# Expert layer: first weight tiles rounded between the logit copies, logits turned ahead of tokens, last rows copied by two engines, output in eight pieces

## The chip, the cores and the metric

The kernel is one program on one core of a Trainium2 chip. The core has a matrix engine (TensorE, PE), a vector engine (VectorE, DVE), a scalar engine (ScalarE, ACT), GpSimd (POOL) and SyncE (SP), whose queue issues all transfers here. Each engine takes its instructions in program order, and they wait for each other by semaphores. TensorE writes to PSUM, eight banks of 128 x 512 fp32 values. The metric is the time of one execution on the device in microseconds (us), less is better.

## What is computed

A decoder of six layers on x (2 x 1024 tokens of 256 features): linear attention, cross attention to a context, a recurrence, causal attention, cross attention, and a layer of eight experts. Only the last matters here:

```python
x = inputs.reshape(G, S, Mm)                 # 8 groups of 256 tokens, 256 features
logits = jnp.einsum('GSM,ME->GSE', x, router_w)          # 8 experts
dispatch, combine = _gating_top2(logits, C)              # softmax, two best experts, 64 slots
expert_inputs = jnp.einsum('GSEC,GSM->EGCM', dispatch, x)
layer_w0 = jnp.einsum('EGCM,EMH->EGCH', expert_inputs, w0_kernel)     # H = 1368
layer_w1 = jnp.einsum('EGCM,EMH->EGCH', expert_inputs, w1_kernel)
hidden = jax.nn.gelu(layer_w0, approximate=True) * layer_w1
expert_outputs = jnp.einsum('EGCH,EHM->EGCM', hidden, wo_kernel)
out = jnp.einsum('EGCM,GSEC->GSM', expert_outputs, combine)           # added to x
```

`inputs` is the layer-normalised residual stream, and the result is added to that stream.

## The kernel before

Everything lies with features on partitions and tokens along the row; `c.xT` is the residual stream, two feature halves (FT = 2) by 2048 tokens. All that follows is `expert_layer`. Its order is written out by hand, engine by engine; there is no scheduler.

**Router.** For each of four chunks of 512 tokens `flat_logits` multiplies the normalised tokens by the router's weights into a bank of 8 rows, ScalarE copies them to `flat` (`copy_flat`), and `turn_logits` transposes them so that tokens are on partitions. VectorE reads the turned logits of all chunks at once and makes softmax and two choices in small steps (`do`), with one Exp by ScalarE; two groups of matmuls (`table`) count how many tokens chose an expert before, and the slot codes follow.

**Tokens.** Meanwhile each pair of token tiles is transposed (`turn_x`, eight pairs), rounded by ScalarE to the matrix format (`split_tokens`, into `tok_high`), and the remainder is made by TensorE (`leave_rest`) and copied by ScalarE (`rest_of_tokens`, `tok_rest`). High part and rest together keep fp32 precision.

**Gather.** For each 128 tokens VectorE writes a one-hot tile in two operations (L3161 and L3163, `one_part` and `one_hot`, double-buffered by group). For each of eight groups of 256 tokens `gather` multiplies them with tokens (L2834, four matmuls for each of two feature halves), and ScalarE copies the slots (L3065, L3067). The first gather needs the codes and the rest of all tokens.

**Weights.** An expert's weights come in three parts by SyncE's queue, those of expert 0 at the layer's start. ScalarE rounds a tile of w0 and w1 (`split_w`, L2991, 128 x 512), and GpSimd subtracts to get the rest (`rest_of_w`, L2794). Five tiles (AHEAD = 5) are done ahead of the loop. SyncE asks for the next expert's first part once GpSimd has subtracted the fourth tile.

**Loop.** 88 units (8 experts, 11 tiles of the hidden dimension): `widen` (12 matmuls, L2885), Gelu by ScalarE, product by VectorE, rounding by ScalarE and rest by GpSimd, and two units later `narrow` (6 matmuls, L2898). Besides, pairs of experts are combined in two banks used in turn (`ring_bank`): tiles called `e` are an expert's output transposed to slots (two for each expert), `y` are their products with the turned gates, added to `c.xT` by VectorE (L3203).

**Tail.** After the last expert come the tiles of `last`: two `e` tiles (L2910), each copied by VectorE in two halves of 64 rows (L3214, rows of the two experts interleaved), and eight `y` tiles (L2922), of four token ranges q by two feature halves m. Each `y` first waits for the copy of the second `e` tile, and for its bank to have been read. SyncE stores each 512 tokens (both halves, 512 KB) when its second sum has been added.

The program's names: `psum` banks, `arena` a shared buffer (normalised tokens, `flat`, slots, `e_out`), `m_...` the tiles of this layer.

Of the kernel before, what the change touches and what calls it, by code (L numbers as in the profile page):

```python
# [25 lines left out]
ACT = mybir.ActivationFunctionType  # L26
# [5 lines left out]
FT = D // P  # L32
CH = 512
# [26 lines left out]
EXP, HID, CAP, GR = 8, 1368, 64, 8  # L60
# [2581 lines left out]
def expert_layer(nc, c):  # L2642
# [3 lines left out]
    PAIRS = EXP // 2  # L2646
    GP = GR // 2
# [5 lines left out]
    AHEAD, W_RING = 5, 6  # L2653
# [24 lines left out]
    with ExitStack() as ctx:  # L2678
# [4 lines left out]
        e = c.signals(nc, "e", dict(made=0, read=0, w0_done=0, w1_done=0, gelu=0, hidden=0, h_high=0, h_rest=0, comb=0, combined=0,  # L2683
                                       narrowed=0, out_copied0=0, out_copied1=0, x_high=0, x_rest=0, w_high=0, w_rest=0, o_high=0,
                                       o_rest=0, w_loaded0=0, w_loaded1=0, w_loaded2=0, wo_loaded0=0, wo_loaded1=0, wo_loaded2=0,
                                       stored=0, router=0))
        set_round(0, s, e)
        w_loaded = [e[f"w_loaded{g}"] for g in range(len(PARTS))]
        wo_loaded = [e[f"wo_loaded{g}"] for g in range(len(PARTS))]
# [23 lines left out]
        router = sb("m_router", [P, FT, EXP])  # L2713
# [41 lines left out]
        with nc.Block() as block:  # L2755

            @block.sync
            def _(sync):
                at = c.mats["router"][0]
                sync.dma_start(router[:].rearrange("p k e -> p (k e)"), c.weights_dram[:, at:at + FT * EXP]).then_inc(e["router"].sem, 16)  # L2760
                for g in range(len(PARTS)):
                    load_first(sync, 0, g)
                    load_last(sync, 0, g)
                for ex in range(1, EXP):
                    for g in range(len(PARTS)):
                        sync.wait_ge(*e["w_rest"](HT * (ex - 1) + PARTS[g][-1] + 1))
                        load_first(sync, ex, g)
                        sync.wait_ge(*e["o_rest"](HT * (ex - 1) + PARTS[g][-1] + 1))
                        load_last(sync, ex, g)
                for q in range(GP):  # L2770
                    sync.wait_ge(*e["read"](nth["y", PAIRS - 1, q, FT - 1] + 1))
                    sync.dma_start(c.out[:, :, q * CH:(q + 1) * CH], c.xT[:, :, q * CH:(q + 1) * CH]).then_inc(e["stored"].sem, 16)
                sync.wait_ge(*e["stored"](GP * 16))

            @block.gpsimd
            def _(pool):
# [34 lines left out]
            def _(pe):  # L2811
# [4 lines left out]
                def tile(what):  # L2816
                    n = nth[what]
                    if n >= BANKS:
                        pe.wait_ge(*e["read"](n - BANKS + 1))
                    return ring_bank(what)  # L2820

                def gather(g, m):
# [29 lines left out]
                def turn_x(t2):  # L2852
                    if t2 >= TURNS:
                        pe.wait_ge(*s["x_high"](t2 - TURNS + 1))
                    for t in (0, 1):
                        for k in range(FT):
                            mm = pe.transpose(turn_bank(t2)[:, t * D + k * P:t * D + (k + 1) * P],  # L2857
                                              tokens(k, 2 * t2 + t), c.ident[:])
                    mm.then_inc(s["turned"].sem)

                def leave_rest(t2):

                    pe.wait_ge(*s["x_high"](t2 + 1))
                    if t2 >= 2:
                        pe.wait_ge(*s["x_rest"](t2 - 1))
                    pe.matmul(rest_bank(t2), minus[:], two(tok_high, t2), start=True, stop=False)
                    for t in (0, 1):
                        for k in range(FT):
                            mm = pe.matmul(rest_bank(t2)[:, t * D + k * P:t * D + (k + 1) * P],  # L2869
                                           tokens(k, 2 * t2 + t), c.ident[:],  # L2870
                                           start=False, stop=(t == 1 and k == FT - 1))
                    mm.then_inc(s["x_left"].sem)
# [29 lines left out]
                def fill(what):  # L2902
                    bank = tile(what)
                    if what[0] == "e":
                        _, ex, i = what
                        for m in range(FT):
                            pe.wait_ge(*out_copied[m](ex + 1))
                        for q in (0, 1):
                            for m in range(FT):
                                mm = pe.transpose(bank[:, q * D + m * P:q * D + (m + 1) * P],  # L2910
                                                  out_t[:, m, (2 * i + q) * P:(2 * i + q + 1) * P], c.ident[:])
                    elif what[0] == "back":
                        _, j, q = what
                        pe.wait_ge(*e["combined"](j + 1))
                        for t in range(4):
                            mm = pe.transpose(bank[:, t * P:(t + 1) * P], comb[:, 4 * q + t, :], c.ident[:])  # L2916
                    else:
                        _, j, q, m = what
                        pe.wait_ge(*e["read"](nth["e", 2 * j + 1, 1] + 1))
                        for i in range(2):  # L2920
                            g = 2 * q + i
                            mm = pe.matmul(bank[:, i * D:(i + 1) * D], e_out[:, g, m * P:(m + 1) * P],  # L2922
                                           back[:, g * 2 * P:(g + 1) * 2 * P], start=True, stop=True)
                    mm.then_inc(e["made"].sem)
# [14 lines left out]
                turn_x(0)  # L2939
                for j in LATE:  # L2940
                    flat_logits(j)
                for t2 in range(1, 3):
                    turn_x(t2)
                    if t2 == 1:
                        pe.wait_ge(*s["negated"](1))
                    leave_rest(t2 - 1)
                for j in LATE:
                    turn_logits(j)
                for t2 in range(3, 6):
                    turn_x(t2)  # L2950
                    leave_rest(t2 - 1)
                pe.wait_ge(*s["consts"](2))
# [32 lines left out]
            def _(act):  # L2985
                def split_w(n):
                    ex, h = divmod(n, HT)
                    act.wait_ge(*w_loaded[part_of(h)](2 * 16 * (ex + 1)))
                    if n >= W_RING:
                        act.wait_ge(*e["w1_done"](n - W_RING + 1))  # L2990
                    act.activation(w_high[:, n % W_RING, :, :, 0:H_N(h)], raw_of(n), ACT.Copy).then_inc(e["w_high"].sem)  # L2991
# [38 lines left out]
                def copy_flat(j):  # L3030
                    act.wait_ge(*s["flat"](j + 1))
                    act.activation(flat[:, j * CH:(j + 1) * CH], c.bank(j % 2)[0:EXP, :], ACT.Copy).then_inc(s["flat_copied"].sem)

                def split_tokens(t2):
                    act.wait_ge(*s["turned"](t2 + 1))
                    act.activation(two(tok_high, t2), turn_bank(t2), ACT.Copy).then_inc(s["x_high"].sem)

                def rest_of_tokens(t2):
                    act.wait_ge(*s["x_left"](t2 + 1))
                    act.activation(two(tok_rest, t2), rest_bank(t2), ACT.Copy).then_inc(s["x_rest"].sem)  # L3040

                copy_flat(0)
                copy_flat(1)
                split_tokens(0)
                copy_flat(2)
                copy_flat(3)
                for t2 in (1, 2):
                    split_tokens(t2)
                    rest_of_tokens(t2 - 1)
                act.wait_ge(*s["step"](2))  # L3050
                act.activation(tab["raw"][:], tab["raw"][:], ACT.Exp).then_inc(s["step"].sem)
                for t2 in range(3, TIL // 2):
                    split_tokens(t2)
                    rest_of_tokens(t2 - 1)
                rest_of_tokens(TIL // 2 - 1)
                for n in range(AHEAD):
                    split_w(n)
                for g in range(GR):
                    for m in range(FT):
                        n = FT * g + m  # L3060
# [11 lines left out]
                for n in range(UNITS):  # L3072
# [12 lines left out]
                    if ex + 1 < EXP and h == 6:  # L3085
                        split_x(ex + 1)
                copy_out(EXP - 1)

            @block.vector
            def _(dve):  # L3090
# [107 lines left out]
                def empty(what):  # L3198
                    of = tile(what)
                    if what[0] == "y":  # L3200
                        _, j, q, m = what
                        x = c.xT[:, m, q * CH:(q + 1) * CH]
                        dve.tensor_tensor(x, of, x, ALU.add).then_inc(e["read"].sem)  # L3203
                    elif what[0] == "back":
                        _, j, q = what
                        dve.tensor_copy(back[:, q * CH:(q + 1) * CH], of).then_inc(e["read"].sem)
                    else:

                        _, ex, i = what
                        of = of.rearrange("p (q n) -> p q n", q=2)  # L3210
                        to = e_out[:, 4 * i:4 * i + 4, :].rearrange("p (q g) n -> p q g n", g=2)
                        for side in range(2):
                            rows = slice(side * CAP, (side + 1) * CAP)
                            ins = dve.tensor_copy(to[rows, :, side ^ (ex % 2), :], of[rows])  # L3214
                        ins.then_inc(e["read"].sem)
# [283 lines left out]
```

## Time and profile before

| | us |
|---|---|
| median of three runs | 1656.48 |
| lowest and highest | 1653.85, 1660.80 |
| profiled execution, its own time | 1651.91 |
| its span in the profile | 1650.2 |
| TensorE busy in the span | 1533.0 (93%) |
| VectorE busy | 962.3 (58%) |
| ScalarE busy | 718.6 (44%) |
| GpSimd busy | 372.2 (23%) |

Times in the views are microseconds from the start of the span. A matmul's record overlaps the next one's, since they are pipelined; the chain of waits shows their share without overlap. "Idle before" is how long an engine did nothing before a row, with what ended it. The granted clock is a share of TensorE's full 2.4 GHz. The expert layer runs from 1175 us to the end.

### The profile page before, as it was taken

The page shows a single profiled execution, that of the slowest core. Times are in us where ns is not written, and L with a number is a line of the kernel's source. Part 1 is how long each engine was busy: PE and PEld are TensorE (multiplying, and loading weights), DVE is VectorE, ACT ScalarE, POOL GpSimd, SP SyncE. Part 2 cuts the span into 40 slices and gives each one's busy share as a digit, 9 for nine tenths or more (in the row PEclk, how much of TensorE's full clock was granted, in tenths as well). Part 3 has the DMA queues.
Part 4 walks back from the last instruction along what each step waited for, and adds up shares of the span by engine and source line. Part 5 has one row for each costly group of instructions (what it writes and reads, how often), then busy time and mean ns, then how long its engine had stood idle before and what let it go on. Part 6 is the DMA issues. An engine that isn't in the chain of part 4 may idle for free. (4 is left out here: it accounts for less than half of the span.)

```text
span 1650.2 us, 19104 instructions
## 1 busy us (share of the span) xinstructions
PE 1533.0 (93%) x6998; PEld 838.9 (51%) x7002; DVE 962.3 (58%) x1491; ACT 718.6 (44%) x1256; POOL 372.2 (23%) x300
## 2 busy tenths in 40 slices
PE   6989999998999999977999999889879999999998
PEld 3744444432222234434454544332358888888886
DVE  4642124767675652343978776368579575564753
ACT  4345232453334333251466566533555444545441
POOL 0000000122221210034200000110216655655561
PEclk9989999999999999987999999989999999999998
DMA  6000000000000000017255330000302332312201
GB/s 274 1 1 0 0 0 4 1 0 1 1 0 1 1 0 0 0 68 98 28 128 67 40 40 2 1 4 1 103 26 77 98 100 73 103 65 88 84 9 51
DMA packets 38707, 67.54 MB, mean 41 GB/s; under 512 B 3864, under 2 KB 19288, under 8 KB 38232
## 3 DMA queue, kind: packets, MB, share of 16 engines
q1 hardware_dynamic: 38616, 66.33, 15.6%
q8 instruction: 56, 0.92, 0.2%
q14 instruction: 35, 0.29, 0.1%
HBM read 57.80 MB, written 8.39 MB: 40 GB/s over the span
## 5 line engine op out<-in xcount | busy, mean ns | idle before, releaser
L1994 ACT ACTIVATE arena<-psum 128x512 f32<-128x512 f32 (+3 forms) x384 | 164.8, 498 | 131.0 <-PE psum L1863 97.5
L2051 DVE TENSOR_REDUCE b_mx<-psum 128x1 f32<-128x512 f32 (+3 forms) x304 | 181.3, 653 | 44.3 <-PE psum L1841 34.8
L2794 POOL TENSOR_TENSOR m_w_rest<-m_w,m_w_high 128x512 fp32r<-128x512 f32 (+1 forms) x88 | 112.6, 1281 | 159.4 <-ACT m_w_high L2991 159.4
L3230 DVE TENSOR_TENSOR m_hidden<-m_gelu,psum 128x512 f32<-128x512 f32 (+1 forms) x88 | 60.4, 686 | 143.6 <-ACT m_gelu L3079 122.5
L2885 PE MATMUL psum<-m_x_high,m_w_high 128*128 128x512 f32 (+1 forms) x352 | 137.2, 390 | 2.9 <-issue 2.9
L2885 PE MATMUL psum<-m_x_rest,m_w_high 128*128 128x512 f32 (+1 forms) x352 | 137.0, 389 | 0.0
L2885 PE MATMUL psum<-m_x_high,m_w_rest 128*128 128x512 f32 (+1 forms) x352 | 137.0, 389 | 0.0
L2800 POOL TENSOR_TENSOR m_h_rest<-m_hidden,m_h_high 128x512 fp32r<-128x512 f32 (+1 forms) x88 | 122.0, 1387 | 58.0 <-ACT m_h_high L3005 58.0
L1203 ACT ACTIVATE x_probs<-psum 128x1024 f32<-128x1024 f32 x64 | 65.5, 1023 | 135.9 <-PE psum L955 135.9
L1346 DVE TENSOR_REDUCE x_mx<-psum 128x2 f32<-128x1024 f32 x64 | 77.0, 1219 | 51.2 <-PE psum L929 51.1
L3079 ACT ACTIVATE m_gelu<-psum 128x512 f32<-128x512 f32 (+1 forms) x88 | 52.4, 596 | 119.0 <-PE psum L2885 119.0
L1838 PE MATMUL psum<-b_k_stack,b_q_stack 96*128 96x512 bf16 (+3 forms) x288 | 89.4, 341 | 6.5 <-POOL weights_sb L1770 3.7
L1860 PE MATMUL psum<-b_q_stack,b_k_stack 98*128 98x512 bf16 (+3 forms) x288 | 90.0, 331 | 5.4 <-DMA b_q_stack<-b_stage 3.1
L3005 ACT ACTIVATE m_h_high<-m_hidden 128x512 fp32r<-128x512 f32 (+1 forms) x88 | 55.7, 633 | 81.5 <-DVE m_hidden L3230 81.5
L968 PE MATMUL psum<-x_probs,arena 128*64 128x512 f32 x256 | 71.0, 633 | 8.5 <-ACT x_out L1213 8.5
L955 PE MATMUL psum<-arena 64*128 64x512 f32 x256 | 74.8, 662 | 0.0
L2885 PEld LDWEIGHTS psum<-m_x_high,m_w_high 128*128 128x128 f32 (+1 forms) x352 | 65.0, 185 | 17.9 <-issue 3.2
L1875 PE MATMUL psum<-arena,weights_sb 128*32 128x512 f32 (+3 forms) x768 | 73.3, 500 | 0.0
L2885 PEld LDWEIGHTS psum<-m_x_high,m_w_rest 128*128 128x128 f32 (+1 forms) x352 | 65.0, 185 | 15.0
L2885 PEld LDWEIGHTS psum<-m_x_rest,m_w_high 128*128 128x128 f32 (+1 forms) x352 | 65.0, 185 | 14.9
L2898 PE MATMUL psum<-m_h_high,m_o_high 128*128 128x512 f32 (+1 forms) x176 | 72.3, 411 | 0.2 <-POOL m_h_rest L2800 0.2
L2898 PE MATMUL psum<-m_h_high,m_o_rest 128*128 128x512 f32 (+1 forms) x176 | 68.8, 391 | 0.0
(546 smaller groups left out, 3008.1 us busy)
## 6 DMA issues: line engine op xcount, KB each, us to landing
m_w<-w SPq DMA_DIRECT2D x32, 512.0 KB, 4.6
m_wo<-wo SPq DMA_DIRECT2D x16, 512.0 KB, 3.9
weights_sb<-weights SPq DMA_DIRECT2D x2, 2820.0 KB, 12.2
m_w<-w SPq DMA_DIRECT2D x16, 344.0 KB, 5.0
b_q_stack<-b_q_dram SPq DMA_DIRECT2D x36, 128.0 KB, 6.8
b_k_stack<-b_k_dram SPq DMA_DIRECT2D x36, 128.0 KB, 7.3
weights_sb<-weights SPq DMA_DIRECT2D x1, 3328.0 KB, 13.6
b_q_dram<-b_q_parts SPq DMA_DIRECT2D x6, 512.0 KB, 3.7
```

What stands on the lines that cost most here:

```text
L955: mm = pe.matmul(to[0:keys, h, :], k, qt[b][rows, m, half * CH:(half + 1) * CH], start=False, stop=True)
L968: mm = pe.matmul(out_tile[h * DH:(h + 1) * DH, :], v, probs[slot % RING][0:keys, h, :], start=(kt == 0), stop=(kt == TT))
L1346: dve.tensor_reduce(mx[:, n % 2, i // 2, i % 2, :], two_heads(tile(("piece", n, i))), AX, ALU.max).then_inc(s["read"].sem)
L1838: mm = pe.matmul(bank[:, x * keys:(x + 1) * keys], qs[n % 3][0:ROWS, h, qi * P:(qi + 1) * P], ks[n % 3][0:ROWS, h, first:first + keys], st ...
L1860: mm = pe.matmul(score(slot)[:, 0:n], ks[a][0:ROWS + SHIFT, h, ki * P:(ki + 1) * P], qs[a][0:ROWS + SHIFT, h, q0:q0 + n], start=True, stop ...
L1875: mm = pe.matmul(out_tile[h * PAD:(h + 1) * PAD, CH - n:CH], v_aug[:, b * TT + ki, quad * QUAD + h, :], probs[(QUAD * (2 * pair + i) + h) ...
L1994: act.activation(probs[slot % RING][:, 0:n], score(slot)[:, 0:n], ACT.Exp, scale=SCALE).then_inc(s["expd"].sem)
L2051: dve.tensor_reduce(mx[:, part, qi, heads[0]:heads[0] + nh], tile(("piece", p))[:, 0:nh * keys].rearrange("p (h n) -> p h n", n=keys), AX, ...
L2794: pool.tensor_tensor(w_rest[:, n % W_RING, :, :, 0:H_N(n % HT)], raw_of(n), w_high[:, n % W_RING, :, :, 0:H_N(n % HT)].bitcast(F32), ALU.s ...
L2800: pool.tensor_tensor(h_rest[rows, n % H_RING, :], hidden[rows, n % 2, :], h_high[rows, n % H_RING, :].bitcast(F32), ALU.subtract).then_inc ...
L2885: mm = pe.matmul(c.bank(base + n % 2)[0:H_N(h), :], of[:, k, :], x_of[ex % 2][:, k, :], start=(k == 0 and i == 0), stop=(k == FT - 1 and i ...
L2898: mm = pe.matmul(total(m), of[rows, n % O_RING, m * P:(m + 1) * P], h_of[rows, n % H_RING, :], start=(h == 0 and i == 0), stop=(h == HT - ...
```

## The change

Five weight tiles are rounded by ScalarE between the logit copies instead of behind the last token copy. TensorE turns the last logits right after the second turn of tokens. In the tail, ScalarE copies rows 64 to 127 of the last two `e` tiles, with a semaphore `half_read` of its own, and a product waits only for the `e` tile that it reads. The output is stored in eight pieces, one for each `y` tile. Nothing of the arithmetic changes.

```diff
@@ SyncE
-                    sync.wait_ge(*e["read"](nth["y", PAIRS - 1, q, FT - 1] + 1))
-                    sync.dma_start(c.out[:, :, q * CH:(q + 1) * CH], c.xT[:, :, q * CH:(q + 1) * CH]).then_inc(e["stored"].sem, 16)
-                sync.wait_ge(*e["stored"](GP * 16))
+                    for m in range(FT):
+                        sync.wait_ge(*e["read"](nth["y", PAIRS - 1, q, m] + 1))
+                        sync.dma_start(c.out[:, m, q * CH:(q + 1) * CH], c.xT[:, m, q * CH:(q + 1) * CH]).then_inc(e["stored"].sem, 16)
+                sync.wait_ge(*e["stored"](GP * FT * 16))
@@ TensorE, a bank for a tile
                         pe.wait_ge(*e["read"](n - BANKS + 1))
+                        if what[0] == "y" and what[1] == PAIRS - 1 and what[2] == 0:
+                            pe.wait_ge(*e["half_read"](what[3] + 1))
@@ TensorE, a y tile
-                        pe.wait_ge(*e["read"](nth["e", 2 * j + 1, 1] + 1))
+                        pe.wait_ge(*e["read"](nth["e", 2 * j + 1, q // 2] + 1))
+                        if j == PAIRS - 1:
+                            pe.wait_ge(*e["half_read"](q // 2 + 1))
@@ TensorE, router
-                for t2 in range(1, 3):
-                    turn_x(t2)
-                    if t2 == 1:
-                        pe.wait_ge(*s["negated"](1))
-                    leave_rest(t2 - 1)
+                turn_x(1)
                 for j in LATE:
                     turn_logits(j)
-                for t2 in range(3, 6):
+                pe.wait_ge(*s["negated"](1))
+                leave_rest(0)
+                for t2 in range(2, 6):
                     turn_x(t2)
                     leave_rest(t2 - 1)
@@ ScalarE, router
                 copy_flat(1)
+                for n in range(2):
+                    split_w(n)
                 split_tokens(0)
+                split_w(2)
                 copy_flat(2)
+                split_w(3)
                 copy_flat(3)
-                for t2 in (1, 2):
-                    split_tokens(t2)
-                    rest_of_tokens(t2 - 1)
+                split_w(4)
+                split_tokens(1)
+                rest_of_tokens(0)
+                split_tokens(2)
+                rest_of_tokens(1)
...
-                for n in range(AHEAD):
-                    split_w(n)
@@ ScalarE, tail
                 copy_out(EXP - 1)
+                for what in last[:2]:
+
+                    _, ex, i = what
+                    act.wait_ge(*e["made"](nth[what] + 1))
+                    rows = slice(CAP, 2 * CAP)
+                    to = e_out[:, 4 * i:4 * i + 4, :].rearrange("p (q g) n -> p q g n", g=2)
+                    act.activation(to[rows, :, 1 ^ (ex % 2), :], ring_bank(what).rearrange("p (q n) -> p q n", q=2)[rows], ACT.Copy)\
+                       .then_inc(e["half_read"].sem)
@@ VectorE, an e tile
-                        for side in range(2):
+                        for side in range(1 if ex == EXP - 1 else 2):
```

ScalarE's queue in the router, of the kernel before, from the first two logit copies (`arena<-psum 8x512`) to Exp (`m_raw`):

```order
L3032 ACTIVATE arena<-psum 8x512 x2
L3036 ACTIVATE m_tok_high<-psum 128x512
L3032 ACTIVATE arena<-psum 8x512 x2
L3036 ACTIVATE m_tok_high<-psum 128x512
L3040 ACTIVATE m_tok_rest<-psum 128x512
L3036 ACTIVATE m_tok_high<-psum 128x512
L3040 ACTIVATE m_tok_rest<-psum 128x512
L3051 ACTIVATE m_raw<-m_raw 128x128
```

The same stretch of the changed kernel, whose line numbers are 3 to 9 higher:

```order
L3035 ACTIVATE arena<-psum 8x512 x2
L2994 ACTIVATE m_w_high<-m_w 128x512 x2
L3039 ACTIVATE m_tok_high<-psum 128x512
L2994 ACTIVATE m_w_high<-m_w 128x512
L3035 ACTIVATE arena<-psum 8x512
L2994 ACTIVATE m_w_high<-m_w 128x512
L3035 ACTIVATE arena<-psum 8x512
L2994 ACTIVATE m_w_high<-m_w 128x512
L3039 ACTIVATE m_tok_high<-psum 128x512
L3043 ACTIVATE m_tok_rest<-psum 128x512
L3039 ACTIVATE m_tok_high<-psum 128x512
L3043 ACTIVATE m_tok_rest<-psum 128x512
```

Five `m_w_high` stand ahead of the second token tile; Exp still comes after two `m_tok_rest`. TensorE's queue of the kernel before, from the last two chunks' logits (`m_router`) to the turned logits (`128x8`):

```order
L2843 MATMUL psum<-arena,m_router 8x512 x4
L2857 MATMUL psum<-ident,arena 128x128 x4
L2866 MATMUL psum<-m_tok_high,m_minus 128x512
L2869 MATMUL psum<-ident,arena 128x128 x4
L2857 MATMUL psum<-ident,arena 128x128 x4
L2866 MATMUL psum<-m_tok_high,m_minus 128x512
L2869 MATMUL psum<-ident,arena 128x128 x4
L2849 MATMUL psum<-ident,arena 128x8 x8
```

And of the changed kernel, the same matmuls:

```order
L2846 MATMUL psum<-arena,m_router 8x512 x4
L2860 MATMUL psum<-ident,arena 128x128 x4
L2852 MATMUL psum<-ident,arena 128x8 x8
L2869 MATMUL psum<-m_tok_high,m_minus 128x512
L2872 MATMUL psum<-ident,arena 128x128 x4
L2860 MATMUL psum<-ident,arena 128x128 x4
L2869 MATMUL psum<-m_tok_high,m_minus 128x512
L2872 MATMUL psum<-ident,arena 128x128 x4
```

The turned logits pass two groups of `leave_rest` (a matmul with `m_minus` and four with tokens) and one turn of tokens.

## Rows read from the trace of the kernel before

**Rows 1.** The page's first line: span and number of instructions.
```profile
span 1650.2 us, 19104 instructions
```

**Rows 2.** Windows: busy time (x records) by engine, granted clock, DMA share, GB/s.
```profile
1190.00:1195.00 5.00, 5.00 (x37) 3.67 (x35) 0.00 (x0) 2.86 (x6) 0.00 (x0) 1.00 0.00 0
1215.00:1220.00 5.00, 3.94 (x10) 2.63 (x9) 4.86 (x8) 1.32 (x4) 1.37 (x1) 0.50 0.67 210
1240.00:1640.00 400.00, 396.33 (x1804) 325.94 (x1803) 248.51 (x402) 186.05 (x364) 225.68 (x171) 0.99 0.22 72
1638.00:1640.00 2.00, 2.00 (x6) 1.62 (x5) 0.99 (x2) 0.00 (x0) 0.00 (x0) 0.50 0.00 0
```

**Rows 3.** Timeline, TensorE, 1200 to 1237: start, us, operation, count, idle before.
```profile
1201.45 0.46 PE L2955 MATMUL psum<-m_m,m_before 128*128 128x128 f32 x2 [1.45 <-DVE m_t L3136]
...
1208.70 0.47 PE L2834 MATMUL psum<-m_one_hot,m_tok_high 128*128 128x512 f32 x1 [1.07 <-DVE m_one_hot L3163]
...
1213.94 0.47 PE L2834 MATMUL psum<-m_one_hot,m_tok_high 128*128 128x512 f32 x1 [3.18 <-DVE m_one_hot L3163]
...
1224.37 0.47 PE L2834 MATMUL psum<-m_one_hot,m_tok_high 128*128 128x512 f32 x1 [0.74 <-issue]
...
1231.48 0.47 PE L2834 MATMUL psum<-m_one_hot,m_tok_high 128*128 128x512 f32 x1 [0.28 <-issue]
...
1236.39 0.47 PE L2885 MATMUL psum<-m_x_high,m_w_high 128*128 128x512 f32 x1 [2.85 <-issue]
```

**Rows 4.** One line's instructions: count, shortest/median/longest in ns, first and last start.
```profile
L3161 DVE TENSOR_SCALAR arena<-m_iota,m_code x16: 476/481/1509, 1206.1 to 1230.1; 128x512 f32<-128x512 f32 x16
```
```profile
L3163 DVE SCALAR_TENSOR_TENSOR m_one_hot<-m_iota,m_code,arena x16: 750/752/1689, 1206.7 to 1230.6; 128x512 fp32r<-128x512 f32 x16
```

**Rows 5.** Timeline of VectorE: the normalising, and three rows of the gather.
```profile
1185.25 2.50 DVE L3111 TENSOR_TENSOR arena<-arena 128x512 f32<-128x512 f32 x4 [3.94 <-ACT arena L3028]
...
1209.03 1.69 DVE L3163 SCALAR_TENSOR_TENSOR m_one_hot<-m_iota,m_code,arena 128x512 fp32r<-128x512 f32 x1
...
1221.81 0.49 DVE L3161 TENSOR_SCALAR arena<-m_iota,m_code 128x512 f32<-128x512 f32 x1 [1.33 <-PE psum L2834]
```

**Rows 6.** Timeline of GpSimd, the five subtractions ahead of the loop.
```profile
1208.87 7.50 POOL L2794 TENSOR_TENSOR m_w_rest<-m_w,m_w_high 128x512 fp32r<-128x512 f32 x5 [30.75 <-ACT m_w_high L2991]
```

**Rows 7.** Timeline of ScalarE: the last residue copy before Exp, and the roundings.
```profile
1194.60 0.60 ACT L3040 ACTIVATE m_tok_rest<-psum 128x512 fp32r<-128x512 f32 x1 [0.48 <-PE psum L2869]
...
1208.17 2.70 ACT L2991 ACTIVATE m_w_high<-m_w 128x512 fp32r<-128x512 f32 x5
```

**Rows 8.** Chain of waits in the router: start, us without overlap, what.
```profile
1191.28 0.59 PE psum L2857 x4
...
1194.57 0.60 PE psum L2849 x8
...
1196.16 0.32 ACT m_raw L3051
```

**Rows 9.** Timeline of the tail, all engines.
```profile
1631.26 0.60 ACT L3017 ACTIVATE m_out_t<-psum 128x512 f32<-128x512 f32 x1 [3.17 <-PE psum L2898]
...
1632.76 2.81 DVE L3214 COPY arena<-psum 64x512 f32<-64x512 f32 x4 [0.81 <-PE psum L2910]
...
1635.72 10.25 PE L2922 MATMUL psum<-arena 128*128 128x256 f32 x32 [2.56 <-DVE arena L3214]
1637.80 0.69 DVE L3203 TENSOR_TENSOR xT<-psum,xT 128x512 f32<-128x512 f32 x1 [2.23 <-PE psum L2922]
...
1642.18 0.69 DVE L3203 TENSOR_TENSOR xT<-psum,xT 128x512 f32<-128x512 f32 x1 [0.27 <-PE psum L2922]
...
1646.01 0.69 DVE L3203 TENSOR_TENSOR xT<-psum,xT 128x512 f32<-128x512 f32 x1 [0.27 <-PE psum L2922]
```

**Rows 10.** DMA issues: count, KB each, median us from issue to landing.
```profile
out<-xT SPq DMA_DIRECT2D x4, 512.0 KB, 3.1
...
x_cx<-ctx_t SPq DMA_DIRECT2D x1, 128.0 KB, 2.2
```

More of the change, by code:

```diff
@@ L2685, in expert_layer @@
                                        o_rest=0, w_loaded0=0, w_loaded1=0, w_loaded2=0, wo_loaded0=0, wo_loaded1=0, wo_loaded2=0,
-                                       stored=0, router=0))
+                                       stored=0, router=0, half_read=0))
         set_round(0, s, e)
```

## The prediction

> **What bounds the kernel now.** I read the page's span first [rows 1], then the windows [rows 2]: from 1240 to 1640 us TensorE is busy 396.33 of 400 us. That loop over experts is at its bound, and nothing in the change takes a matmul out of it. The time can move only where TensorE waits: in the router and gather ahead of the loop (1186 to 1236 us) and in the tail (after 1631 us). So I read the timelines of both, engine by engine.
>
> The router is one chain: logits turned, a row of small VectorE steps with one Exp by ScalarE among them, slot codes, then 16 pairs of VectorE operations (L3161, L3163) that write the one-hot tiles, two pairs for each of the eight gathers by TensorE. Ahead of the last four gathers VectorE sets the pace: gathers 4 and 7 start at 1224.37 and 1231.48 us [rows 3], so (1231.48 - 1224.37) / 3 = 2.37 us for each. Their eight matmuls stand 0.31 us short of that. Gather 0 starts at 1208.70, so at this pace gather 7 would start at 1208.70 + 7 x 2.37 = 1225.29. It starts 6.19 us later.
>
> The rows say why. L3161 takes 476 to 481 ns mostly and 1509 at most, L3163 750 and 1689 [rows 4]; the long ones are those from 1209.03 on [rows 5], exactly while GpSimd does its first five subtractions L2794 (1208.87, 7.50 us in all) [rows 6]. Those wait for ScalarE's five roundings of weights, L2991, which stand behind the last copy of tokens (1208.17 us, 2.70 us) [rows 7]. Then TensorE, left waiting, runs at a granted clock of 0.50, its 1.2 GHz level, between 1215 and 1220 us [rows 2], and VectorE in turn idles 1.33 us at 1221.81 for it [rows 5].
>
> **Part 1, five weight tiles rounded earlier.** ScalarE's five L2991 move between the logit copies, to about 1186.7 us on. Each takes 2.70 / 5 = 0.54 us of queue; the gaps ahead of the logit copies hold them, except that the last stands ahead of the second token tile. GpSimd can then subtract from about 1187.4: five of 7.50 / 5 = 1.50 us at most, over by 1195. In the gather VectorE keeps its short durations. Gain: the 6.19 us above. The other half of the double buffer has to follow: the pair for gather 2 waits for gather 0's matmuls, 2.06 us after 1208.70, and in my timetable it wants to start only 0.1 us after that; the rows of gathers 4 to 7 have the same order and keep 2.37 us. I take the full 6.19; the lower bound, if only the durations shrink and the clock still falls, is 6.19 - 1.33 = 4.86.
>
> What do the moved subtractions hit? VectorE's normalising, L3111, ends at 1187.75 (1185.25 + 2.50) [rows 5]; then it idles until the logits. With logits at 1192.5 (part 2) three small steps stand before Exp, about 1 us. Were each held for as long as L3161's worst excess (1509 - 481 = 1028 ns) Exp's input would be ready at 1196.6; but GpSimd is through by 1195, so it is ready by 1195.5 at the latest, and Exp isn't reached before 1195.7 (below). Cost 0. If that cover goes, it costs up to 0.9 us.
>
> The weights must have landed. No DMA moves between 1190 and 1195 us [rows 2], so all have; ScalarE wants the first at 1186.7. A landing as late as 1190 would cost up to 3.3 us; the first megabyte of 5.3 requested is in my view there long before. Cost 0. SyncE, which waits on GpSimd's fourth subtraction, asks for expert 1's first weights some 20 us earlier; nobody waits for the queue then.
>
> **Part 2, logits turned ahead of tokens.** Before, two residue groups and a turn of tokens stood ahead of the last turned logits, from the end of the turn at 1191.87 to 1194.57 [rows 8]: 2.70 us. Now the last logits are turned at 1192.47. But Exp, which the chain needs next, stands on ScalarE behind two token copies and two residue copies. The last of these waits for TensorE's second residue group, which now ends at 1194.57 + 0.60 = 1195.17 (the turned logits ahead of it). That copy started at 1194.60 before [rows 7]; now it starts at 1195.20, and Exp some 0.52 behind it, at 1195.72 instead of 1196.16 [rows 8]. **Gain 0.44, not 2.70.** TensorE's work up to the counts is the same sum and ends at 1200.0, as before (1201.45 less 1.45 idle) [rows 3]; VectorE's steps now reach the counts at 1200.9, so the 0.44 survives. Bounds: 0 (ScalarE loses 0.4 to the queue) and 1.45 (TensorE is the limit).
>
> From gather 7 to the first widening matmul lie 1236.39 - 1231.48 = 4.91 us [rows 3]: same operations, same order, unchanged. **Ahead of the loop: 6.19 + 0.44 = 6.6 us.**
>
> **Part 3, last rows by two engines.** Before, VectorE makes four copies, 2.81 us from 1632.76 [rows 9], and TensorE's last products start at 1635.72. Now VectorE copies rows 0 to 63 and ScalarE rows 64 to 127 of each bank. ScalarE's comparable copy of 128 x 512 takes 0.60 us [rows 9], shorter than VectorE's 2.81 / 4 = 0.70, so VectorE's first ends last, 1633.46. The first product needs only the first bank: it starts at 1633.60. **Gain 2.12.** No row shows both engines reading one bank at once; if they took turns each bank would cost 0.6 more, and 1.5 of the 2.12 is left; I take 0 for that, as the halves are different partitions. The memory page bears on it: by the Trainium skill (PSUM — Partial Sum Buffer, on bank collisions) two engines may be in one bank at once when they are in different 32-partition quadrants, which these are; no run here shows it, and by that rule the sum would be the one I take.
>
> Second, the clock. TensorE stood idle before 1635.72 and ran at 0.50 at 1638 to 1640 [rows 2]. The first sum was read 2.08 us after the start (1637.80), against half of that, 1.04, at 2.4 GHz; and after 1642.18 the sums are read every (1646.01 - 1642.18) / 4 = 0.96 us [rows 9]. With the idle 2.56 us cut to about 0.4 I expect no fall: start to last read is 1.04 + 7 x 0.96 = 7.76 instead of 10.29. **Gain 2.5**; the lower bound is 0, if it falls all the same.
>
> **Part 4, output in eight.** After the last addition (1646.70) 3.5 us are left. 512 KB land in 3.1 us; the nearest smaller one, 128 KB, in 2.2 [rows 10]. A piece of 256 KB by the straight line: 2.5. **Gain 0.6**, between 0 and 0.9. The issue, about 0.55 us before, fits into the 0.96 between sums. Removing one wait and adding two on TensorE (`half_read`) queues nothing else behind them.
>
> **Sum.** 6.19 + 0.44 + 2.12 + 2.53 + 0.6 = 11.9 us. The profiled execution has 1651.91 us (span 1650.2), so it would come to 1640.0. The median of the three runs shown is 1656.48, 4.6 higher; its terms are the same, so I take off the same: **1644.6 us**, 0.72% less.
>
> **Rivals.**
> *The tail's clock falls all the same.* For it: part of the idle time ahead of it stays. Against: its longest stretch, 2.56 us, goes. Gain 9.4: 1647.1 us. 15%.
> *The clock falls ahead of the loop instead.* TensorE idles 2.85 us before the first widening, and no fall shows there now, but a slightly longer one at 1213.94 (3.18 us) did bring one [rows 2, 3]; the shift of all by 6.6 us may do it. Half speed for about as long as it lasted, 6.6 us, costs 3.3: 1647.9 us. 8%.
> *The collision moves with the subtractions.* If ScalarE or the weights are late, GpSimd's five land in the small VectorE steps: 5 x 1.03 = 5.1 back, 1649.7 us. Against: the idle from 1187.75 to 1192.5. 7%. By the Trainium skill (SBUF — State Buffer, "Who interferes with whom") a VectorE operation with two SBUF inputs, or a fast copy or tensor_scalar, and a GpSimd one hold the shared port for a whole instruction, and a reduction never does. L3161's 1509 against 481 ns agrees. By it only the subtraction of the maxima would be held before Exp, and the result is as in part 1; were the five late, fewer than five steps would be held and the loss is smaller than 5.1.
> *Slower: the weights' landing becomes the bound.* ScalarE is in order, so a wait for weights now stops logits and tokens behind it, where it stopped nothing before. Each microsecond past 1186.7 goes on the chain. It eats the whole gain from a landing at 1198.6 on; at 1204 the kernel takes 1661.9 us. Against: DMA is idle by 1190. 2%.
> *The turning does nothing,* ScalarE's queue holding Exp altogether: 1645.0, inside my own range.
>
> **How the numbers follow.** Forecast with small misses of its terms 63%, clock in tail 15, clock before the loop 8, collision 7, slower 2, the rest (5) for a median of three runs that themselves spread over 7 us. About 0.5%, 8.3 us, is what a measurement of this kernel can tell; the line stands at 1648.2. Faster by more: 63 + 15 + most of 8, less a few for the spread: 0.81. Within: 0.17. Slower: 0.02. Low end: forecast less the 1 us that TensorE's slack would allow and some 3 of spread, 1640.5. High end: the collision case, 1650.
>
> **What would show it.** Right: all 16 pairs in the gather near 0.48 and 0.75 us; gathers 2.37 apart at clock 1.00; GpSimd's first five over before Exp; logits read 2.7 us earlier but Exp only 0.4; last products starting 2.1 us sooner, relative to the last narrowing; sums 0.96 apart throughout. Wrong: long L3161 rows anywhere, a gap on TensorE before gather 2, Exp gaining the whole 2.7, ScalarE's half-copies slower than 0.7 us, or clock 0.50 in either place.

## Result and profile after

The changed kernel takes 1643.88 us (median of ten runs, 1637.78 to 1649.77), the kernel before 1655.07 (ten runs, 1649.85 to 1661.16). The ratio of the runs is 0.9936, 95% interval 0.9916 to 0.9955; of 1655.07 us that is 10.6 us less (7.4 to 13.9), while the two medians alone differ by 11.2. The forecast was 1644.6 and 11.9 us less.

The profiled executions differ by only 8.0 us (span 1642.2 against 1650.2), because the changed kernel reaches its expert layer 4.1 us later, in code that is the same. In the recurrence, 390 to 510 us, the granted clock was 1.00 before and is 0.92 and 0.94 now. Counted by VectorE's instructions, which are the same in both, the changed kernel falls 8.5 us behind in this stretch, and regains a part of it later. The windows of the kernel before, and below them of the changed kernel (busy time and count of five engines, granted clock, DMA share, GB/s):

```profile
390.00:450.00 60.00, 53.86 (x254) 15.72 (x252) 46.15 (x49) 19.72 (x21) 11.82 (x6) 1.00 0.00 1
450.00:510.00 60.00, 57.93 (x254) 16.28 (x252) 42.39 (x45) 21.05 (x22) 14.64 (x7) 1.00 0.00 1
```
```profile
390.00:450.00 60.00, 54.30 (x238) 15.43 (x236) 42.56 (x45) 17.03 (x17) 9.85 (x5) 0.92 0.00 0
450.00:510.00 60.00, 58.36 (x238) 15.97 (x238) 39.21 (x42) 19.49 (x20) 14.10 (x6) 0.94 0.00 1
```

So I count from the first router matmul (1182.48 us before, 1186.57 now). All numbers are differences between starts in the timelines, in us:

| stretch | before | changed | difference | forecast |
|---|---|---|---|---|
| router to VectorE's read of the logits | 12.71 | 10.02 | -2.69 | -2.7 |
| router to Exp | 13.68 | 13.40 | -0.28 | -0.44 |
| router to gather 0 | 26.22 | 25.92 | -0.30 | -0.44 |
| gather 0 to gather 7 | 22.78 | 16.58 | -6.20 | -6.19 |
| gather 7 to the first widening | 4.91 | 4.94 | 0.03 | 0 |
| loop, to the last unit's narrowing | 393.21 | 393.22 | 0.01 | 0 |
| to the first product | 6.12 | 4.11 | -2.01 | -2.12 |
| to the last sum's start | 10.29 | 7.75 | -2.54 | -2.53 |
| to the end of the span | 4.19 | 3.11 | -1.08 | -0.6 |
| router to the end of the span, the sum | 467.72 | 455.63 | -12.09 | -11.9 |

The first rows answer [rows 3 to 5]. One line of the changed kernel each, L3176 and L3178 (count, shortest/median/longest in ns), and VectorE's three steps before Exp:

```profile
L3176 DVE TENSOR_SCALAR arena<-m_iota,m_code x16: 478/480/486, 1209.9 to 1227.7; 128x512 f32<-128x512 f32 x16
```
```profile
L3178 DVE SCALAR_TENSOR_TENSOR m_one_hot<-m_iota,m_code,arena x16: 750/751/752, 1210.5 to 1228.2; 128x512 fp32r<-128x512 f32 x16
```
```profile
1196.59 0.29 DVE L3129 COPY m_logits<-psum 128x128 f32<-128x128 f32 x1 [4.75 <-PE psum L2852]
1196.91 0.29 DVE L3132 TENSOR_REDUCE m_mx<-m_logits 128x16 f32<-128x128 f32 x1
1197.23 0.81 DVE L3133 TENSOR_TENSOR m_raw<-m_logits,m_mx 128x128 f32<-128x128 f32 x1
1200.37 0.29 DVE L3136 TENSOR_REDUCE m_sm<-m_raw 128x16 f32<-128x128 f32 x1 [2.33 <-ACT m_raw L3060]
```

No long one-hot operation is left. Beside GpSimd's subtractions now stand these steps instead: the row of GpSimd's timeline below (it answers [rows 6]) ends at 1197.90, and the one step with two inputs in SBUF, L3133, took 0.81 instead of 0.29 us, while the copy from PSUM and the reduction kept 0.29. It cost nothing: after it VectorE still waited 2.33 us for Exp. By the Trainium skill (SBUF — State Buffer, "Who interferes with whom") just this kind of step contends with a GpSimd instruction that reads SBUF, and a reduction never does; the trace agrees, with these numbers.

```profile
1191.40 6.50 POOL L2795 TENSOR_TENSOR m_w_rest<-m_w,m_w_high 128x512 fp32r<-128x512 f32 x5 [9.19 <-ACT m_w_high L2994]
```

ScalarE's queue around Exp (its L3060), answering [rows 7, 8], and the chain of waits there:

```profile
1197.91 0.60 ACT L3043 ACTIVATE m_tok_rest<-psum 128x512 fp32r<-128x512 f32 x1 [0.91 <-PE psum L2872]
1198.40 0.59 ACT L3039 ACTIVATE m_tok_high<-psum 128x512 fp32r<-128x512 f32 x1
1199.47 0.60 ACT L3043 ACTIVATE m_tok_rest<-psum 128x512 fp32r<-128x512 f32 x1 [0.48 <-PE psum L2872]
1199.97 0.30 ACT L3060 ACTIVATE m_raw<-m_raw 128x128 f32<-128x128 f32 x1
```
```profile
1195.96 0.59 PE psum L2852 x8
1196.55 0.43 PE psum L2869
...
1199.47 0.60 ACT m_tok_rest L3043
1200.07 0.20 ACT m_raw L3060
```

Exp starts right behind the second residue copy, with its input long there. The tail, answering [rows 9, 10]; ScalarE's and VectorE's half copies start together, and the clock holds:

```profile
1630.40 1.28 DVE L3229 COPY arena<-psum 64x512 f32<-64x512 f32 x2 [0.81 <-PE psum L2913]
1632.48 0.69 DVE L3218 TENSOR_TENSOR xT<-psum,xT 128x512 f32<-128x512 f32 x1 [0.80 <-PE psum L2927]
```
```profile
1630.40 1.08 ACT L3101 ACTIVATE arena<-psum 64x512 f32<-64x512 f32 x2 [0.91 <-PE psum L2913]
```
```profile
1632.00:1636.00 4.00, 4.00 (x19) 2.83 (x18) 2.77 (x4) 0.00 (x0) 0.00 (x0) 1.00 0.36 137
1636.00:1640.00 4.00, 3.05 (x14) 2.03 (x12) 2.77 (x4) 0.00 (x0) 0.00 (x0) 1.00 0.74 279
```
```profile
out<-xT SPq DMA_DIRECT2D x8, 256.0 KB, 2.0
```

### The profile page after: what moved, and what is told of

Same layout as the page of the kernel before. It is cut to its first block and busy times, and to the rows that moved or that the text cites. A ratio compares the mean times of both kernels' runs of the same rounds, so it can differ in the third digit from the quotient of the medians.

```text
span 1642.2 us, 19114 instructions
## 1 busy us (share of the span) xinstructions
PE 1530.5 (93%) x7002; PEld 835.0 (51%) x7002; DVE 957.0 (58%) x1489; ACT 719.7 (44%) x1258; POOL 371.3 (23%) x300
```

## Experiments

My theory: GpSimd's subtractions beside the one-hot operations cost 6.2 us; the early logits are held by ScalarE's queue; the tail gained by shorter copies and, separately, by the clock. The rivals stand in each expectation. Times of timed runs are compared with runs of the kernel before on the same chip. Five of the kernels (logits alone, output alone, subtractions late, tail kept busy, Exp moved up) have one execution each: they are read from their traces, by stretches, and their whole times say nothing.

**One part at a time.** First the roundings alone: ScalarE's lines of the diff ahead of this, TensorE's order and the tail left as before.

> The kernel before with one part of the change alone: the five roundings of weights stand between the logit copies; the logits are turned where they were, the tail is the old one. Theory (GpSimd's five subtractions hold VectorE's one-hot operations, and that starves TensorE until its clock falls): gather 0 to gather 7 takes 16.6 us instead of 22.8 (a gain of 6.2), all one-hot operations stay near 0.48 and 0.75 us, the clock stays 1.00, and the time is 0.996 of that before. The path up to gather 0 is unchanged or up to 0.3 us longer, since a rounding stands ahead of the second token tile. Rival (the gain in front comes from the logits being turned early): gather 0 to gather 7 stays within 0.5 us of 22.8, and the time stays at 1.000.

Gather 0 to gather 7 took 16.57 us, router to gather 0 26.22, as before; ratio 0.9959 (0.9934 to 0.9984). This part is the larger one, and the rival falls. Two other stretches differ in this profile, though nothing was changed in them: the loop took 394.84 us and not 393.2, and the tail's products 9.27 and not 10.29; more on both below.

The logits alone:

```diff
-                for t2 in range(1, 3):
-                    turn_x(t2)
...
-                    leave_rest(t2 - 1)
+                turn_x(1)
                 for j in LATE:
                     turn_logits(j)
+                pe.wait_ge(*s["negated"](1))
+                leave_rest(0)
...
```

> The kernel before with only the logits turned ahead of the token groups on TensorE. Theory: VectorE reads the logits 2.7 us earlier after the first logit matmul, but Exp on ScalarE stands behind the second residue copy and comes only 0.3 to 0.5 us earlier, as do the counts and gather 0; gather 0 to gather 7 stays at 22.8 us with the long one-hot operations. Rival (Exp follows the logits): Exp 2.7 us earlier, counts 1.4 us earlier, where TensorE is the limit.

Logits at 10.02, Exp at 13.40, gather 0 at 25.94, gather 0 to 7 in 22.33 us. As the theory has it.

The tail copies alone (ScalarE's, VectorE's and TensorE's lines of the tail, output in four):

> The kernel before with only the new tail copies: ScalarE copies rows 64 to 127 of the last two transposed tiles, a product waits only for its own tile, output in four pieces as before. Theory: last narrowing to first product 4.1 us instead of 6.1 (gain 2.0), first product to last sum read 7.8 instead of 10.3 (gain 2.5, the clock stays 1.00), last read to the end unchanged at 4.2; together 4.5 us, 0.997 of the time before. Rival (the clock falls in the tail whenever the idle stretches add up, and stayed up in the changed kernel by chance): gain 2.0 only and the clock at 0.50 in the products.

Narrowing to first product 4.11 us, products 7.75, end 4.15; ratio 0.9978 (0.9954 to 1.0003), an interval that takes in no change, so the 4.5 us rest on the trace. In this run the clock fell elsewhere: the loop took 396.09 us.

The output alone:

```diff
-                    sync.wait_ge(*e["read"](nth["y", PAIRS - 1, q, FT - 1] + 1))
-                    sync.dma_start(c.out[:, :, q * CH:(q + 1) * CH], c.xT[:, :, q * CH:(q + 1) * CH]).then_inc(e["stored"].sem, 16)
+                    for m in range(FT):
+                        sync.wait_ge(*e["read"](nth["y", PAIRS - 1, q, m] + 1))
+                        sync.dma_start(c.out[:, m, q * CH:(q + 1) * CH], c.xT[:, m, q * CH:(q + 1) * CH]).then_inc(e["stored"].sem, 16)
```

> The kernel before with only the output stored in eight pieces. Theory: from the start of the last sum to the end of the span 3.1 us instead of 4.2 (issue 0.33 instead of 0.53, landing 2.0 instead of 3.1); the rest of the tail as before, products at clock 0.50 for about 6 us. Rival (the last piece queues behind the one ahead of it, and only the faster tail made the changed kernel's end short): 3.7 us or more.

From the last sum to the end of the span it takes 3.10 us, with the old slow tail ahead of it (products in 10.12). So the 1.1 us belong to the piece's size.

**Is it GpSimd's subtraction, or ScalarE's queue?** The changed kernel, with one wait more:

```diff
+                pool.wait_ge(*s["one"](2))
                 for n in range(AHEAD):
                     rest_of_w(n)
```

> The changed kernel, in which GpSimd starts its five subtractions only once the first pair of one-hot tiles is written, as in the kernel before; ScalarE's roundings stay early. Theory (the subtractions beside the one-hot operations are the cause, and ScalarE's order is not): one-hot operations of 1.5 to 1.7 us return, the clock falls, and gather 0 to gather 7 takes 21 to 23 us instead of 16.6. Rival (ScalarE's roundings between token copies and slot copies were the cause, since slot copies free the banks): it stays at 16.6 us.

Gather 0 to 7 took 22.90 us, though ScalarE had rounded early. GpSimd's subtractions and VectorE's one-hot operations in this run:

```profile
1208.00 7.65 POOL L2795 TENSOR_TENSOR m_w_rest<-m_w,m_w_high 128x512 fp32r<-128x512 f32 x5 [30.28 <-DVE m_one_hot L3179]
```
```profile
1207.83 0.48 DVE L3177 TENSOR_SCALAR arena<-m_iota,m_code 128x512 f32<-128x512 f32 x1
1208.35 1.66 DVE L3179 SCALAR_TENSOR_TENSOR m_one_hot<-m_iota,m_code,arena 128x512 fp32r<-128x512 f32 x1
1209.93 1.49 DVE L3177 TENSOR_SCALAR arena<-m_iota,m_code 128x512 f32<-128x512 f32 x1
```

The first long operation is the first one that starts after GpSimd has (1208.35 against 1208.00); the one that was already running kept its 0.48 us. That settles the cause: the overlap in time, and not ScalarE's order. Nor are transfers a rival for the long operations: in the kernel before, four of them fill this window, GpSimd is busy throughout, and no DMA moves (the share before the last number is 0.00):

```profile
1210.00:1215.00 5.00, 1.82 (x8) 1.19 (x7) 4.96 (x4) 1.96 (x6) 5.00 (x5) 0.96 0.00 0
```

The loss in the gather has two parts. In each of the six profiles with late subtractions five one-hot operations are long, and they last 4.7 to 4.8 us more in sum than short ones. In the profile with the output alone, gather 0 to 7 took 21.33 us, which is 16.57 and just this sum, although the clock fell there too. In the other five it took 1.0 to 1.6 us more, which is what is left for TensorE at the lower clock.

**Is the tail's slowness the clock?** The kernel before, with TensorE kept at work:

```diff
                 for what in last:
+                    if what == ("y", PAIRS - 1, 0, 0):
+                        pe.wait_ge(*e["gelu"](UNITS))
+                        for _ in range(10):
+                            pe.matmul(c.bank(0), w_high[:, 0, 0, 0, :], x_high[1][:, 0, :], start=True, stop=True)
                     fill(what)
```

> The kernel before with ten more matmuls of 128 x 512 on TensorE between the last transposes and the first product, into a bank that nobody reads; all else as before. Theory (idle time of TensorE lowers its clock in the tail): the products still start 6.1 us after the last narrowing begins, but the clock stays 1.00 there, and the first product to the last sum read takes 7.8 us instead of 10.3. Rival (the products are slow for another reason, such as VectorE's reads or the last copies): 10.3 us as before.

The products start 6.14 us after the narrowing, as before, and take 7.75. TensorE's timeline, and a window at clock 1.00:

```profile
1638.78 2.54 PE L2985 MATMUL psum<-m_x_high,m_w_high 128*128 128x512 f32 x10
1641.59 7.71 PE L2922 MATMUL psum<-arena 128*128 128x256 f32 x32 [0.27 <-DVE arena L3218]
```
```profile
1640.00:1644.00 4.00, 3.73 (x16) 2.68 (x15) 2.50 (x5) 0.00 (x0) 0.00 (x0) 1.00 0.00 0
```

Ten matmuls that nobody reads bring 2.5 us: TensorE's idle time was the cause, and the slow copies mattered by making it. This is one execution, but the other profiles agree: the clock was at 0.50 in the products in all four with the old tail and nothing in its wait, and at 1.00 up to the last sum in all seven with the new tail.

**What the early logits could be worth.** The changed kernel, with Exp moved up on ScalarE:

```diff
                 rest_of_tokens(0)
+                act.wait_ge(*s["step"](2))
+                act.activation(tab["raw"][:], tab["raw"][:], ACT.Exp).then_inc(s["step"].sem)
                 split_tokens(2)
                 rest_of_tokens(1)
-                act.wait_ge(*s["step"](2))
-                act.activation(tab["raw"][:], tab["raw"][:], ACT.Exp).then_inc(s["step"].sem)
```

> The changed kernel with Exp on ScalarE ahead of the third token copy and the second residue copy. Theory (ScalarE's queue kept the early logits from helping): Exp about 1.5 us earlier than in the changed kernel, counted from the first logit matmul, and the counts and gather 0 about 1.1 earlier, since TensorE's own work then is the limit (no idle time ahead of the counts). Rival (Exp's input was late, not its queue): Exp and gather 0 within 0.3 us of the changed kernel.

Exp at 11.83 (1.57 earlier than in the changed kernel), counts at 17.41 instead of 18.67, gather 0 at 24.59 instead of 25.92: 1.3 us, where I expected about 1.1. Then also the counts:

```diff
-                turn_x(6)
-                leave_rest(5)
                 pe.wait_ge(*s["cum2"](1))
...
                 mm.then_inc(s["cnt"].sem)
+                turn_x(6)
+                leave_rest(5)
                 turn_x(7)
...
                         pe.wait_ge(*s["codes"](2))
+                    if n == 2:
                         pe.wait_ge(*s["x_rest"](TIL // 2))
```

> As the one with Exp ahead, and the matmuls of the second choice's counts stand ahead of the seventh turn of tokens, and the first gather no longer waits for the rest of the last tokens (the second one does). Theory: TensorE has no idle stretch left up to the first gather, which starts 1.9 us earlier than in the changed kernel; the gathers stay 2.37 us apart, so the loop starts 1.9 us earlier, and the time is 0.9925 of that before, against 0.9936 of the changed kernel. Rival (gathers are then held by the last residue copies): gather 1 waits and 1 us or less is gained.

Gather 0 at 23.48 us, 2.44 earlier than in the changed kernel, where I expected 1.9, and gather 0 to 7 in 16.54. Ratio to the kernel before 0.9909 (0.9882 to 0.9935).

**The wait ahead of the loop.** On top of that, ScalarE rounds the first half of expert 0's tokens sooner:

```diff
+                        if g == GR - 1:
+                            act.wait_ge(*s["gathered"](n + 1))
+                            act.activation(x_high[0][:, m, :], x_slots[m][:, 0, :], ACT.Copy).then_inc(e["x_high"].sem)
-                act.wait_ge(*s["gathered"](GR * FT))
-                split_x(0)
```

> As the one with Exp and counts ahead, and ScalarE rounds the first half of expert 0's tokens as soon as the last gather's first half is copied, instead of behind the second half. Theory: the stretch from gather 7's start to the first widening matmul is 4.3 us instead of 4.93, so TensorE idles 2.2 us there instead of 2.85; a loop of 393.2 us (clock 1.00 from the start) becomes likelier against 394.8. Rival (something else, such as the rounding of the output weights or the table load of Gelu, ends that wait): 4.9 us as before.

The stretch is 4.57 us instead of 4.93, a little over half of the gain I expected; TensorE idles 2.48 us there, and the clock fell all the same; the loop took 394.82. Ratio 0.9904 (0.9873 to 0.9934). Then the gap filled:

```diff
+                pe.wait_ge(*e["w_high"](1))
+                for _ in range(8):
+                    pe.matmul(c.bank(5), minus[:], w_high[:, 0].rearrange("p w k n -> p (w k n)"), start=True, stop=True)
                 pe.wait_ge(*s["gathered"](GR * FT))
```

> As the one before it, with eight more matmuls of 128 x 512 on TensorE (1.8 us at full clock, into a bank that nobody reads) in the wait ahead of the loop. Theory (the loops of 394.8 and 396.1 us are those in whose first microseconds the clock is at its lower level, since TensorE idled ahead of them): the clock is 1.00 there and the loop takes 393.2 us; the time is at or below that of the kernel with Exp and counts ahead, 0.990 of that before. Rival (the longer loops have another cause): 394.8 or more stays possible with clock 1.00 at the start.

The loop took 393.22 us. Windows of TensorE early in the loop without the fill (the loop starts at 1225.58 us), and below with it (from 1227.42); busy, granted clock, DMA:

```profile
1228.00:1232.00 4.00, 4.00 (x14) 0.73 0.00 0
```
```profile
1228.00:1232.00 4.00, 4.00 (x19) 1.00 0.00 0
```

That the fill did it is not shown: this is one profile, and in four of the eleven kernels without the fill the loop took 393.2 us too. The rival, a longer loop at clock 1.00, didn't come.

It ran at 1638.50 us (six runs, 1635.48 to 1642.05), ratio 0.9899 (0.9872 to 0.9926). These last three can't be told from each other by their times, nor surely from the changed kernel (0.9936, 0.9916 to 0.9955, whose interval meets theirs); by the trace, router to end of span takes 455.63 us in the changed kernel and 452.75 in this last one.

## Why the prediction was right, point by point

**The bound.** The loop is full; it took 393.2 us in both profiles, and nothing moved there between these two.

**The sum.** The profiles give 12.1 us for the 11.9 of the forecast, and that this is so near is in part luck: parts 2 and 3 brought 0.25 us less than forecast and part 4 0.48 more.

**Part 1** came out as worked: 6.20 for 6.19. The pair for gather 2, which had 0.1 us to spare in my timetable, didn't wait: VectorE has no idle time in the gather, and the gathers start 2.42, 2.32 and then 2.36 or 2.37 us apart. What the subtractions hit instead was one step, by 0.52 us, and 2.33 us of waiting were left behind it.

**Part 2.** The mechanism was right (2.69 us on the logits, almost none on Exp), the size a little off: 0.28 for 0.44. The step that missed was that the turned logits add 0.60 ahead of the residue groups. They add 0.59, and the residue matmul right behind them takes 0.43 us of the chain where it took 0.24 before. The experiment with Exp moved up shows that the queue on ScalarE was what held it.

**Part 3.** 2.01 for 2.12: the product starts 0.26 us after the end of VectorE's first half copy, where I took 0.14 us. Both engines read one bank at once with no loss: the copies took VectorE 0.67 and 0.68 us, where the same ones took 0.68 to 0.70 alone, and ScalarE 0.58 and 0.59. The clock's 2.54 is for 2.53, and its cause is shown by the filled gap in the tail. Inside it two small misses cancel: the first sum starts 1.14 us after the first product and not 1.04, and the sums follow each other by 0.86 and 1.05 us in turn, 0.94 on average, and not by 0.96.

**Part 4** was the one under-sized term: 1.08 for 0.6, beyond the 0.9 that I gave as its upper bound. The straight line through 128 KB at 2.2 us, a load, and 512 KB put 256 KB at 2.5; stores of 256 KB land in 2.0. Their issue takes 0.33 us instead of 0.53, which I had not counted as it lies behind the last sum.

**The rivals.** A fall of the clock ahead of the loop was given 8%. It is commoner: of the twelve profiled kernels, the loop took 393.2 us in five, 394.8 in six and 396.1 in one. In each of the seven longer ones TensorE's clock was at its lower level for part of the loop's first 8 us, and in none of the others. But it happens with either front, and costs 1.6, in one case 2.9, not 3.3. That it showed neither in the profile of the kernel before nor in that of the changed one is luck. The size of what was saved varies too: with the old front, gather 0 to 7 took 21.33 to 22.95 us, and the old tail's products 9.27 to 10.29, and the time for which the clock stayed low differed between these profiles. With those two terms at their low ends, 21.33 - 16.57 = 4.76 and 9.27 - 7.75 = 1.52, the gain is 0.30 + 4.76 + 2.01 + 1.52 + 1.08 = 9.7 us; the measured 10.6 lies between this and the profile's 12.1. That this is the whole difference is argued, not shown. The collision case came only as that one step, since the subtractions mostly found VectorE idle. The late subtractions of the experiment are another collision, with the one-hot operations: it cost 6.3 us (16.58 to 22.90), 4.7 of them in five long operations. The weights were not late: in all seven profiles with the new order the first rounding starts 4.13 us after the first router matmul, right behind the two logit copies ahead of it.

## What to carry to other kernels

Work off the critical path still has a place in time: ask which operations of other engines get longer beside it (here 0.48 us became 1.5), and move it to where that engine idles; its duration on its own row tells nothing. Reordering one engine brings nothing while another one's queue holds the next step behind older work, so follow the result through every queue up to its use. And a wait of TensorE like those here, of 2.5 to 3 us, can cost twice, by itself and by the clock after it. Matmuls into a bank that nobody reads, put into such a wait, bought back 2.5 us in the tail; ahead of the loop, where 1.6 us were at stake, one profile doesn't show that they did.

## What I had not expected of the hardware

The same code ahead of the expert layer took from 1181.0 to 1188.2 us in twelve profiled executions, which is more than half of what the whole change is worth. In the two that I compared, the clock in the recurrence has a part in it. Differences of a few microseconds in such a kernel are read stretch by stretch, each counted from its own start, and not from whole times.

Once the clock fell behind an idle stretch of 2.48 us. Behind one of 2.85 or 2.86 us, at the same place ahead of the loop, it fell in six profiles and did not in four others. So which of them is hit is not decided by the length alone; what decides it stays open.
